# Ternary and generated feed-forward: unrolled over sequences, one sequence normalised at a time

## The reference, cut to what matters

```
# stage 5, hidden size 512
h = silu(x @ w1.T * s1) * (x @ w2.T * s2)
h = gelu(h @ h1.T * t1)
h = gelu(h @ h2.T * t2)
return h @ w3.T * s3

# stage 4, second half, hidden size 512
h2 = layernorm(hs, ln2_g, ln2_b)
m = gelu_tanh(h2 @ cf.T + cf_b)
return hs + m @ cm.T + cm_b
```

## Time and profile before

| | |
|---|---|
| time, median of 3 runs | 1951.17 us (1947.07 to 1953.35) |
| the profiled execution | 1949.12 us |
| its span, first to last instruction | 1947.4 us |
| TensorE / VectorE / ScalarE / GpSimd busy | 81% / 59% / 42% / 40% of the span |
| mean granted TensorE clock | 0.878 of full speed |
| generated MLP, first to last row | 1036.41 to 1081.87 us |
| ternary feed-forward | 1082.16 to 1239.98 us |

### The profile page before, as it was taken

The page is one execution under the profiler, slowest core; times in us unless marked ns, Lnnn a source line. Parts: engine busy times, 40 slices in busy tenths (PEclk is TensorE's granted clock), DMA queues, the critical chain, the costliest instruction groups (busy, mean ns, idle before and its releaser), DMA issues. The chain is left out here.

```text
span 1947.4 us, 25298 instructions
## 1 busy us (share of the span) xinstructions
PE 1579.7 (81%) x9201; PEld 911.5 (47%) x9222; DVE 1155.9 (59%) x2847; ACT 810.9 (42%) x1178; POOL 788.4 (40%) x832
## 2 busy tenths in 40 slices
PE   3776578799987999299986699799999999995084
PEld 2455456544445777144444477533443433433053
DVE  5665697578856765668863512356666667664102
ACT  4563334156654544236663423254344344340031
POOL 5531444323226655512223523334444444453633
PEclk8778699669997999559998799899999999996587
DMA  2000000100000000200000100000000000005123
GB/s 73 2 2 1 29 0 1 74 1 1 2 1 21 1 1 1 122 1 1 1 1 0 45 0 0 1 1 1 1 1 0 1 0 1 1 1 184 41 64 91
DMA packets 20819, 37.48 MB, mean 19 GB/s; under 512 B 1760, under 2 KB 18144, under 8 KB 19552
## 3 DMA queue, kind: packets, MB, share of 16 engines
q1 hardware_dynamic: 18656, 31.76, 4.7%
q0 software_dynamic: 2048, 4.21, 0.7%
HBM read 26.50 MB, written 9.47 MB: 18 GB/s over the span
## 5 line engine op out<-in xcount | busy, mean ns | idle before, releaser
L1840 DVE CUSTOM_DVE_ANT_0 s_masked_scores<-s_for_max,s_mask_qk 128x128 bf16<-128x128 f32 (+3 forms) x512 | 227.5, 487 | 63.4 <-PE s_for_max L1676 59.9
L2184 POOL TENSOR_TENSOR s_probs_added<-s_probs 128x1024 f32<-128x1024 f32 x64 | 151.4, 2366 | 272.7 <-ACT s_probs L2320 272.7
L1632 POOL TENSOR_SCALAR_AFFINE_SELECT s_probs<-s_probs 128x256 f32<-128x256 f32 x256 | 101.3, 409 | 312.1 <-ACT s_probs L1777 246.4
L2320 ACT ACTIVATE s_probs<-s_scores 128x1024 f32<-128x1024 f32 x128 | 131.1, 1024 | 197.0 <-PE s_scores L2258 197.0
L2344 DVE TENSOR_REDUCE s_negmax<-s_for_max 128x2 f32<-128x1024 f32 x128 | 155.0, 1211 | 83.5 <-PE s_for_max L2232 83.1
L1138 POOL TENSOR_TENSOR s_hidden_lo<-s_hidden,s_hidden_hi 128x512 fp32r<-128x512 f32 x108 | 142.5, 1320 | 119.3 <-ACT s_hidden_hi L1249 119.2
L1676 PE MATMUL s_for_max<-s_k_stack,s_q_stack 32*128 32x128 f32 (+3 forms) x512 | 137.9, 442 | 33.1 <-DVE s_max_wide L1840 26.8
L1676 PEld LDWEIGHTS s_for_max<-s_k_stack,s_q_stack 32*128 32x128 f32 x512 | 69.3, 205 | 169.4 <-DVE s_max_wide L1840 113.7
L2269 PE MATMUL s_pv<-s_probs,s_v 128*64 128x512 f32 x512 | 139.1, 624 | 0.0
L1777 ACT ACTIVATE s_probs<-s_scores 128x1024 f32<-128x1024 f32 x128 | 126.8, 1023 | 21.8 <-PE s_scores L1697 18.2
L2351 DVE RECIPROCAL s_recip<-s_odd_jobs 128x128 f32<-128x128 f32 x128 | 112.3, 920 | 23.5 <-PE s_odd_jobs L2279 23.5
(11 more groups left out here) (425 smaller groups left out, 3632.6 us busy)
## 6 DMA issues: line engine op xcount, KB each, us to landing
s_w<-extra SPq DMA_DIRECT2D x2, 2048.0 KB, 9.8
wbuf<-w SPq DMA_DIRECT2D x1, 3460.0 KB, 11.0
s_probs<-extra SPq DMA_DIRECT2D x1, 2898.0 KB, 10.1
wbuf<-w SPq DMA_DIRECT2D x1, 2888.0 KB, 15.0
wbuf<-w SPq DMA_DIRECT2D x1, 2124.0 KB, 8.0
dispatched<-s_empty_slots SPq DMA_DIRECT2D x1, 2064.0 KB, 15.9
s_rows<-dispatched SPq DMA_DIRECT2D x8, 258.0 KB, 2.6
expert_rows<-s_empty_slots SPq DMA_DIRECT2D x1, 2048.0 KB, 21.6
```

What stands on the lines that cost most here:

```text
L1632: last = nc.gpsimd.affine_select(out=diag, in_=diag, compare_op=ALU.is_ge, fill=0.0, base=0, pattern=[[0, diag.shape[1]], [1, P]], channel ...
L1840: last = nc.vector.tensor_tensor_reduce(out=junk[:, m % 2, at:at + n], in0=p1[m % 2][:, at:at + n], in1=mask[:, S - n:S], scale=1.0, scala ...
L2184: nc.gpsimd.tensor_tensor(added[:, half, :, :], probs[:, g % 2, 2 * half, :, :], probs[:, g % 2, 2 * half + 1, :, :], ALU.add).then_inc(s_ ...
L2320: nc.scalar.activation(probs[:, g % 2, j, :, :], p2[:, :, :], ACT.Exp, scale=dh ** -0.5).then_inc(s_exp, 1)
```

## The change

Both loops are written out in Python instead of `Fori`. Before the first sequence only its own LayerNorm is done; the next one's is spread through the pass of the one before it: VectorE scales sequence c + 1 after f = 0 of sequence c (ternary) or ahead of its loop (MLP), TensorE transposes it after the up products, ScalarE copies it after the silus (ternary) or after the second gelu (MLP). In the ternary stage VectorE makes the low part of c + 1 and the statistics of c + 2 after the last high part of h1. ScalarE makes the high parts of w1 and w2, then copies the first sequence, then makes those of h1, and in the first pass those of h2. GpSimd makes the first rstd, the low parts of w1, w2 and h1, the second rstd, and those of h2 between the low parts of h0 and h1. In the MLP the bias of a sequence is added after its scaling, and VectorE waits for one of them at a time. The helpers `stats_of`, `scaled`, `low_part`, `rstd_of`, `turned` and `copied` were there before.

```diff
--- before.py
+++ after.py
@@ -1369,12 +1369,14 @@
 
         @block.gpsimd
         def _(pool):
-            pool.wait_ge(sh.wsem[stage], 16)
-            split.gpsimd(pool, range(2))
-            ln.gpsimd(pool, lambda c: split.gpsimd(pool, [2 + c]))
-            split.gpsimd(pool, range(2 + n, 2 + 2 * n))
-            with pool.Fori(0, B) as c:
+            ln.rstd_of(pool, 0)
+            split.gpsimd(pool, range(2 + n))
+            for c in range(B):
+                if c + 1 < B:
+                    ln.rstd_of(pool, c + 1)
                 for i, h in enumerate((h0, h1)):
+                    if c == 0 and i == 1:
+                        split.gpsimd(pool, range(2 + n, 2 + 2 * n))
                     for k in range(n):
                         pool.wait_ge(s_hi[i], c * n + k + 1)
                         nc.gpsimd.tensor_tensor(lo[i][:, k, :], h[:, k, :], hi[i][:, k, :].bitcast(F32),
@@ -1385,9 +1387,9 @@
             pe.sem_inc(s_p1, 1)
             pe.sem_inc(s_y, 1)
             pe.wait_ge(sh.wsem[stage], 16)
-            ln.tensor(pe)
+            ln.turned(pe, 0)
             pe.wait_ge(split.s_lo, 2)
-            with pe.Fori(0, B) as c:
+            for c in range(B):
                 pe.wait_ge(ln.s_hi, c + 1)
                 for f in range(n):
                     pe.wait_ge(s_h0, 1 + c * n + (f - 1 if f else 0))
@@ -1399,6 +1401,8 @@
                         nc.tensor.matmul(ps[f % 2][:, :], w_lo[:, fs], ln.hi[:, cols(c)], start=False, stop=False)
                         last = nc.tensor.matmul(ps[f % 2][:, :], w_hi[:, fs], ln.lo[:, cols(c)], start=False, stop=True)
                     last.then_inc(s_up, 1)
+                if c + 1 < B:
+                    ln.turned(pe, c + 1)
                 for i, ps, s_free, s_done in ((0, ps_a, s_h1, s_p1), (1, ps_b, s_h2, s_p2)):
                     layer = split.parts[2 + i * n:2 + (i + 1) * n]
                     for f in range(n):
@@ -1434,13 +1438,18 @@
         @block.scalar
         def _(act):
             act.wait_ge(sh.wsem[stage], 16)
-            split.scalar()
-            ln.scalar(act)
-            with act.Fori(0, B) as c:
+            split.scalar(range(2))
+            ln.copied(act, 0)
+            split.scalar(range(2, 2 + n))
+            for c in range(B):
                 for f in range(n):
                     act.wait_ge(s_up, c * n + f + 1)
                     nc.scalar.activation(silu[:, f % 2, :], ps_a[f % 2][:, :], ACT.Silu,
                                          scale=w["w1_s"][:, f:f + 1]).then_inc(s_silu, 1)
+                if c + 1 < B:
+                    ln.copied(act, c + 1)
+                if c == 0:
+                    split.scalar(range(2 + n, 2 + 2 * n))
                 for s_sum, first, ps, out, scale, s_out in ((s_p1, 1, ps_a, h1, w["h1_s"], s_h1),
                                                             (s_p2, 0, ps_b, h2, w["h2_s"], s_h2)):
                     for f in range(n):
@@ -1454,17 +1463,19 @@
         def _(dve):
             dve.sem_inc(s_h0, 1)
             dve.sem_inc(s_x, 1)
-            ln.vector(dve)
+            ln.stats_of(dve, 0)
+            ln.scaled(dve, 0)
             dve.wait_ge(sh.wsem[stage], 16)
             for k in range(n):
                 nc.vector.tensor_tensor(w3s[:, k, :], w["w3"][:, k * D:(k + 1) * D], w["w3_s"],
                                         ALU.mult).then_inc(s_w3, 1)
-            ln.low_parts(dve)
+            ln.low_part(dve, 0)
+            ln.stats_of(dve, 1)
 
             def high(i, k):
                 nc.vector.tensor_copy(hi[i][:, k, :], (h0, h1)[i][:, k, :]).then_inc(s_hi[i], 1)
 
-            with dve.Fori(0, B) as c:
+            for c in range(B):
                 for f in range(n):
                     dve.wait_ge(s_silu, c * n + f + 1)
                     if f == 0:
@@ -1474,9 +1485,15 @@
                                                    op0=ALU.mult, op1=ALU.mult).then_inc(s_h0, 1)
                     dve.wait_ge(s_h0, 1 + c * n + f + 1)
                     high(0, f)
+                    if f == 0 and c + 1 < B:
+                        ln.scaled(dve, c + 1)
                 for f in range(n):
                     dve.wait_ge(s_h1, c * n + f + 1)
                     high(1, f)
+                if c + 1 < B:
+                    ln.low_part(dve, c + 1)
+                if c + 2 < B:
+                    ln.stats_of(dve, c + 2)
                 dve.wait_ge(s_y, 1 + c + 1)
                 nc.vector.tensor_tensor(sh.x[:, tiles(c), :], sh.x[:, tiles(c), :], ps_y[0][:, :, :],
                                         ALU.add).then_inc(s_x, 1)
@@ -2016,8 +2033,10 @@
 
         @block.gpsimd
         def _(pool):
-            ln.gpsimd(pool)
             for c in range(B):
+                ln.rstd_of(pool, c)
+            for c in range(B):
+                pool.wait_ge(ln.s_xn, (c + 1) * TPC)
                 ts = slice(c * TPC, (c + 1) * TPC)
                 nc.gpsimd.tensor_tensor(sh.x[:, ts, :], sh.x[:, ts, :],
                                         gen["cm_b"].unsqueeze(1).broadcast_to([P, TPC, D]), ALU.add).then_inc(s_bias, 1)
@@ -2025,13 +2044,15 @@
         @block.tensor
         def _(pe):
             pe.sem_inc(s_y, 1)
-            ln.tensor(pe)
-            pe.wait_ge(ln.ready, B)
-            with pe.Fori(0, B) as c:
+            ln.turned(pe, 0)
+            for c in range(B):
+                pe.wait_ge(ln.ready, c + 1)
                 for f in range(n):
                     pe.wait_ge(s_gelu, 1 + c * n + f)
                     nc.tensor.matmul(ps_h[f][:, :], gen["cf_w"][:, f * P:(f + 1) * P], sh.xnT[:, cols(c)],
                                      start=True, stop=True).then_inc(s_h, 1)
+                if c + 1 < B:
+                    ln.turned(pe, c + 1)
                 pe.wait_ge(s_x, 1 + c)
                 for k in range(n):
                     pe.wait_ge(s_gelu, 4 + c * n + k + 1)
@@ -2044,21 +2065,27 @@
         @block.scalar
         def _(act):
             act.sem_inc(s_gelu, 4)
-            ln.scalar(act)
-            with act.Fori(0, B) as c:
+            ln.copied(act, 0)
+            for c in range(B):
                 for f in range(n):
                     act.wait_ge(s_h, c * n + f + 1)
                     if f == 0:
                         act.wait_ge(s_y, 1 + c)
                     nc.scalar.activation(h[:, f, :], ps_h[f][:, :], ACT.Gelu_apprx_tanh,
                                          bias=gen["cf_b"][:, f:f + 1]).then_inc(s_gelu, 1)
+                    if f == 1 and c + 1 < B:
+                        ln.copied(act, c + 1)
 
         @block.vector
         def _(dve):
             dve.sem_inc(s_x, 1)
-            ln.vector(dve)
-            dve.wait_ge(s_bias, B)
-            with dve.Fori(0, B) as c:
+            ln.stats_of(dve, 0)
+            for c in range(B):
+                if c + 1 < B:
+                    ln.stats_of(dve, c + 1)
+                ln.scaled(dve, c)
+            for c in range(B):
+                dve.wait_ge(s_bias, c + 1)
                 dve.wait_ge(s_y, 1 + c + 1)
                 nc.vector.tensor_tensor(sh.x[:, tiles(c), :], sh.x[:, tiles(c), :], ps_y[0][:, :, :],
                                         ALU.add).then_inc(s_x, 1)
```

## The result

| | before | after |
|---|---|---|
| time, median of 5 runs | 1951.52 us (1947.07 to 1953.35) | 1940.40 us (1932.80 to 1943.17) |
| the profiled execution | 1949.12 us, span 1947.4 | 1941.68 us, span 1939.9 |
| stage time, generated MLP | 45.96 us | 38.82 us |
| stage time, ternary | 157.92 us | 152.86 us |
| ternary: first product after VectorE's first row | 20.41 us | 8.09 us |

The ratio is 0.9945 [0.9928, 0.9963]. A stage time here is the distance from VectorE's first row of statistics in the stage to its first one in the next stage, so the MLP's is 1036.41 to 1082.37 before and 1039.32 to 1078.14 after. An up phase goes from its first product to the first one of a layer; the layers with w3 go from there to the next sequence's first product.

The account below looks back on a forecast made before the run. TensorE bounds the MLP's loop, serial preparation the heads, engine hand-offs the ternary up phases. MLP 9.0 - 1.65 = 7.3 plus ternary 12.2 - 8.4 = 3.8 gives 11.1 us off 1951.17: 1940, range 1933 to 1948.

Parts of the forecast that it names:

- MLP, head: Generated MLP before its loop: first product at about 1041.6 instead of 1050.66, 9.0 us gained.
- MLP, loop: Generated MLP's loop: four transposes in the product stream in three of four passes, 0.55 us each, 1.65 lost.
- ternary, head: Ternary stage before its first product: start at 1090.5 instead of 1102.78, 12.2 us gained.
- (a): Ternary, first up phase: second rstd behind four h1 parts delays VectorE; 12.1 us against 9.34, 2.8 lost.
- (b): Ternary up phases of sequences 1 and 2: scalings held by GpSimd's subtraction, 1.9 us each, 3.8 together.
- (c): Ternary: next input's low part pushes back GpSimd's last subtraction, 0.6 us three times, 1.8 lost.
- (d): Ternary: transposes lie in TensorE's 1.56 us wait before the first layer, no cost; without that cover 0.55 each.
- (e): Ternary: ScalarE's second-layer high parts make the first gelu 1 us late; TensorE needs it later, so no cost.
- More comes: Rival, chance 0.20: VectorE and GpSimd don't hold each other; ternary stage gives 8.9, together 16.2 us: 1935.
- Table loads return: Rival, chance 0.05: copies between silu or gelu calls bring table loads, 7.5 us in the MLP: 1947.5.
- The gain stays small: Rival, chance 0.12: later rstd, transposes at 1.1 and code fetch at 0.4 us leave 5.3 gained: 1946.
- Slower: Rival, chance 0.05: TensorE's clock stays low through the ternary layers after up-phase waits, 21 us lost: 1961.

Follow-up runs that it names:

- scale_after_up: Against the kernel after: next sequence's scalings moved behind the whole up phase, its transposes and copies into the first layer; ternary stage 148.78 us.
- loops_only: Against the kernel before: only the loops of both stages written out, old order kept; ratio 0.9986, ternary stage 157.83 us.
- as_changed: The kernel after, unaltered, timed once more on the same chip as two further versions; 1937.39 us, ratio 0.9921 against the kernel before.
- both: Against the kernel after: scalings moved behind the up phase and the input's low part behind the second high part of h1; 1935.12 us, ratio 0.9904.
- scale_before_high: Against the kernel after: next sequence's scalings put ahead of the high part of f = 0; ternary stage 150.25 us.
- rstd_ahead: Against the kernel after: GpSimd makes the second rstd before the four low parts of h1; ternary stage 154.41 us.
- old_split_order: Against the kernel after: ScalarE makes all ten high parts before the first copy, GpSimd three low parts before the first rstd; ternary stage 155.62 us.
- low_early: Against the kernel after: next input's low part put behind the second high part of h1 instead of the last; ternary stage 154.14 us.
- ternary_alone: The kernel after's ternary stage with the kernel before's generated MLP; 1948.85 us, ratio 0.9977, ternary stage 153.96 us.

## Why the prediction was right, step by step

| step | forecast | measured in the profile after |
|---|---|---|
| MLP, head | 9.0 gained | 9.15 |
| MLP, loop | 1.65 lost | 2.06 |
| ternary, head | 12.2 gained | 12.3 |
| (a) first up phase | 2.8 lost | 2.84 |
| (b) two up phases | 1.9 each | 1.7 each |
| (c) three low parts | 0.6 each | 0.4 each |
| (d), (e), straight code | 0 | 0 (`scale_after_up`, the first layers, `loops_only`) |
| sum | 11.1 | 12.2 by stage times |

The steps were right in kind. That 1940 was met within 0.4 us is partly luck: (b) and (c) were taken too dear and the MLP's loop too cheap, which leaves 12.2 by the stages, and the medians happened to lie 11.1 apart. With the same kernel in `as_changed` they lay 17.4 apart (1937.39 against 1954.82).

- *The MLP's loop.* Warm passes have a period of 7.44 instead of 7.00 us, so four transposes cost 0.44, not 0.55. The rest, 1.2 us, is the first pass: 10.36 against 9.18 before. In other profiles of the new MLP that pass took 8.98 to 10.37, according to when the clock rose. The prediction had no term for it.
- *(a)* came by the chain that was forecast: the scalings end 8.23 us after the first product (1094.46; forecast 8.3), f = 3 begins at 8.95 (forecast 9.2), the layer at 12.18 (12.1). The clock's later rise lies under that wait: `as_changed` had 9 long products where the profile after had 10, and its phase is 12.20. But a second chain lies behind the first. With the scalings out of the phase 0.7 of the 2.84 stays (10.04), and by the rows of `both` it is VectorE's high parts held beside GpSimd's late subtractions. The prediction did not have that: it took the parts of h1 as a delay of the rstd only.
- *(b)* rested on rows 4 alone, one stretch of 2.06 us. Rows of after have 2.08 beside one operation of GpSimd and 3.02 beside two, `scale_before_high` has 1.11 for the same four, `rstd_ahead` 4.00 and `old_split_order` 3.99 beside three. The mechanism is shown by experiment; the rival *More comes* needed it away, and falls. The Trainium skill (SBUF — State Buffer, the list under "Reading the diagram") has this as an exclusive lock of a port pair for a whole instruction; these durations agree with it.
- *(c)* is real, but GpSimd's last subtraction is pushed back by less than I took, as the longest wait went from 0.4 to 0.8, not to 1. `low_early` takes it away.
- *Table loads return* falls by the one load in the MLP. *The gain stays small* falls: neither the transposes nor the fetch came dearer. *Slower* did not decide, but its mechanism exists: in 5 of the 14 profiles a second stretch of long products came within the stage, after a wait of TensorE of 1.9 to 3.6 us, at a price of 0.8 (`rstd_ahead`) to 2.2 us (`low_early`, first layers 28.01 against 25.80 in the next pass). I had set it at all or nothing (21 us) on a row of another stage.

What stays open is why it falls in some profiles and not in others. After waited 2.32 us and kept its clock, and so did `as_changed` after 2.61; `ternary_alone` waited 1.88 and lost it. Their code in this stage is the same.

## What to carry to other kernels

When a stage begins with a serial preparation of all its input, do it for the first piece only, and put the pieces' own constants (here split weights) on each engine in the order in which the first piece needs them; the gain can be read before it is built, from the distance between the stage's start and its first product. What is then spread through the loop must be placed beside what the other engines do at that instant: one position later or earlier of four small VectorE operations was worth 1 us a pass here, and a rstd made earlier made things worse. Judge such edits by stage times, for executions of this kernel differ by more than they give, and trust a stage time of one profile to about 1 us only: the clock moved those of unchanged code by 1.1 to 1.4.

## What the hardware showed beyond that

- Beside GpSimd working without a gap VectorE got one scaling through for each of its operations: four of them take 1.11 us alone, 2.05 to 2.08 beside one operation of about 1.27, 3.02 beside two, 3.99 and 4.00 beside three.
- TensorE's clock fell to its 1.2 GHz level within a stage after waits of 1.88 to 3.60 us. The first long product began 0.4 to 1.3 us after TensorE had resumed, so the long products stand at the head of the next work and look like that work's fault.
- Ten filler products ahead of the first transposes and after them (1.63 us for the last three) did not raise it: the next 7 products were long, as many as in `both` without fillers.
